# A two-direction state-space layer on Trainium2: whole-array decay tiles, B and C held once, more buffers, a smaller software DMA space

## The reference

```python
xn = _layernorm(x, axis=-1)
zxbcdt = xn @ in_proj_w.T           # z 2048, x 2048, B 64, C 64, dt 16 columns
def _branch(zxbcdt, conv_w, conv_b, dt_bias, A_log, D, norm_w):
    dt = softplus(zxbcdt[..., -NHEADS:] + dt_bias)
    A = -exp(A_log)
    xBC = silu(causal_conv(xBC, conv_w, conv_b))     # 4 taps over time
    # per head h of 16, head width 128, state width 64:
    #   h_t = h_{t-1} * exp(dt_t * A) + dt_t * x_t B_t ;  y_t = h_t C_t
    y = _ssd_scan(x, dt, A, Bm, Cm) + D * x
    yz = y * silu(z)
    return yz * rsqrt(mean(yz * yz) + EPS) * norm_w
y_fw = _branch(zxbcdt, ...)
y_bw = _branch(zxbcdt[:, ::-1, :], ...)              # the same, time reversed
s = (y_fw + y_bw[:, ::-1, :]) @ out_proj_w.T
g = silu(ffn(xn))     # ffn: 1024 x 1024 matmul, inputs and weights rounded to a 6-bit grid
x = x + s * g
```

## Time and profile before

| | us |
|---|---|
| median of 3 runs | 1595.62 |
| lowest and highest of them | 1593.83, 1722.22 |
| the profiled execution's own time | 1591.32 |
| its span on the slowest core (core 4) | 1589.8 |
| spans of the 8 cores | 1564.6 to 1589.8 |
| PE busy on that core | 1327.5 |
| DVE, ACT, POOL busy | 980.8, 831.1, 710.5 |

### The profile page before, as it was taken

One profiled execution on the slowest core, in us unless ns is written; L12 is line 12 of the kernel. 1 busy time (PEld: TensorE's weight loads), 2 busy tenths in 40 slices (PEclk: granted clock), 3 DMA queues, 4 the chain that ended last, 5 costly groups with the idle time before them and its releaser, 6 DMA issues.

```text
span 1589.8 us, 38392 instructions; the slowest of 8 cores (1564.6 to 1589.8 us)
## 1 busy us (share of the span) xinstructions
PE 1327.5 (84%) x13568; PEld 770.9 (48%) x13568; DVE 980.8 (62%) x1760; ACT 831.1 (52%) x1660; POOL 710.5 (45%) x950
## 2 busy tenths in 40 slices
PE   0677998977999899999896588898988889888995
PEld 0453665555655566656663343444444444444442
DVE  2615877665788876677745665654556655666652
ACT  0235665554656656665665654544445555555540
POOL 2422565543656545556432433453444444343442
PEclk9887998998999999999996699989999989998998
DMA  9793898989987877776688778998999888888862
GB/s 172 164 177 87 198 207 180 166 198 203 188 191 172 184 180 182 187 183 154 154 235 224 180 182 192 224 205 202 201 211 209 217 204 215 210 214 203 209 158 80
DMA packets 447284, 298.03 MB, mean 187 GB/s; under 512 B 321139, under 2 KB 395379, under 8 KB 445558
## 3 DMA queue, kind: packets, MB, share of 16 engines
q1 hardware_dynamic: 444502, 282.44, 75.4%
q0 software_dynamic: 2592, 13.14, 5.4%
HBM read 152.39 MB, written 84.94 MB: 149 GB/s over the span
## 4 chain that ended last, share of the span: by engine, by line
PE 51%; DMA 16%; ACT 10%; issue 9%; DVE 7%; SPq 5%; POOL 1%; DVEq 0%; ACTq 0%; POOLq 0%
PE ps L356 51%; SPq L383 5%; ACT L366 3%; DMA xtm<-cvx 3%; DMA g<-scr 3%; DMA ar<-yz 2%; DMA xt<-xn 2%; ACT e L366 2%; DMA u<-u 2%; DMA ar<-wz 2%; DVE yz L369 2%; DMA scr<-lts 1%; ACT sq L366 1%; DMA lts<-spl 1%; ACT cvx L366 1%
## 5 line engine op out<-in xcount | busy, mean ns | idle before, releaser
L356 PE MATMUL ps<-ar,xt 128*128 128x512 bf16 (+1 forms) x1792 | 379.9, 356 | 118.9 <-DMA xt<-xn 45.2
L356 PEld LDWEIGHTS ps<-ar,xt 128*128 128x128 bf16 x1792 | 148.8, 98 | 315.1 <-issue 172.2
L356 PE MATMUL ps<-xt,ar 128*128 128x256 bf16 x2304 | 277.9, 278 | 19.6 <-ACT stg L366 7.3
L366 ACT ACTIVATE cvx<-ps,cbt 128x256 bf16<-128x256 f32 x512 | 200.7, 474 | 175.5 <-PE ps L356 149.1
L356 PE MATMUL ps<-ar 128*128 128x512 bf16 x1024 | 259.5, 398 | 16.7 <-ACT e L366 12.7
L369 POOL TENSOR_TENSOR stmp<-st,dec 128x1024 f32<-128x1024 bf16 x64 | 132.7, 2074 | 292.0 <-DVE spl L380 120.6
L356 PEld LDWEIGHTS ps<-xt,ar 128*128 128x128 bf16 x2304 | 222.3, 100 | 63.8 <-issue 32.7
L369 DVE TENSOR_TENSOR yz<-ps,sz 128x1024 bf16<-128x1024 f32 x128 | 154.9, 1219 | 40.8 <-PE ps L356 40.5
L366 ACT ACTIVATE sq<-yz 128x1024 bf16<-128x1024 bf16 x128 | 134.9, 1054 | 78.0 <-DVE yz L369 34.8
L356 PE MATMUL ps<-stg,cd 64*64 64x256 bf16 x4096 | 157.8, 296 | 18.5 <-ACT cvx L366 6.6
L356 PEld LDWEIGHTS ps<-ar 128*128 128x128 bf16 x1024 | 95.1, 101 | 151.3 <-issue 59.6
(11 more groups left out here) (92 smaller groups left out, 1684.8 us busy)
## 6 DMA issues: line engine op xcount, KB each, us to landing
u<-u SPq DMA_DIRECT2D x54, 512.0 KB, 5.2
sp_x<-stg SPq DMA_DIRECT2D x64, 256.0 KB, 3.0
g<-scr SPq DMA_DIRECT2D x64, 256.0 KB, 5.3
sp_z<-sz SPq DMA_DIRECT2D x32, 512.0 KB, 4.3
sp_y<-yz SPq DMA_DIRECT2D x32, 512.0 KB, 5.0
sz<-sp_z SPq DMA_DIRECT2D x32, 512.0 KB, 4.5
ar<-sp_y SPq DMA_DIRECT2D x32, 512.0 KB, 4.6
stg<-sp_x SPq DMA_DIRECT2D x60, 259.0 KB, 4.6
```

The source lines that it names most:

```text
L356: return lambda e: e.matmul(out, lhsT, rhs, start=start, stop=stop)
L366: return lambda e: e.activation(out, in_, func, **kw)
```

## The change

1. **Decay tiles over the whole array.** `lts` now holds, per chunk and per half b of the moving tokens, a stationary tile of 128 columns (all 128 output tokens), and `rh` is one tile, not two. A call of `weights` still issues four matmuls, now of 128 stationary columns and 4 heads x 64 tokens = 256 moving columns. The mask is split: within a block of 64 by 64 tokens it stays in rows 64 to 127; the block that is masked altogether gets its -1e30 from two constant rows, 56 and 57. `spl` and the DMA transpose of it are half as wide; the transpose goes to a new tile `ltt`, from which a new DVE copy spreads 56 rows into `lts`. One DMA, not two, writes the rows of `rh`. `LTS.free` no longer waits for the store to `scr`.
2. **B and C once.** The projection gives 128 columns (B, C) in place of 256; the spilled array `sp_bc`, the tile `sbc`, the evacuation, the halo copies, the store and the load are half as large. The convolution's matmuls for them read the one copy, both column halves from the same rows.
3. **Buffers.** `E` 4 (was 3), `GC` 2 (was 1), `YB` 2 (was 1), `YT` 3 (was 2).
4. **Recording order in the second phase.** The load of `sp_y`, the add and the transpose of the sum are taken out of `b_scan` into `b_sum`, which is recorded after the output projection of the previous group.
5. **Software DMA space.** `dynamic_dma_scratch_size=8192` is passed when the program is built.

```diff
+        rh[d, 57 - d] = NEG
+        rh[d, 64:128] = np.tile(m[0:64, 0:64], (1, 2))[:, None, :]
+    c["c_rh"] = rh.reshape(2, 128, NH * 128)
+    lt = np.zeros((128, 2, 2, 128), dtype=BF)
+    lt[57, :, 0, 64:128] = 1.0
+    lt[56, :, 1, 0:64] = 1.0
+    for b in range(2):
+        lt[64:128, :, b, b * 64:(b + 1) * 64] = np.eye(64, dtype=BF)[:, None, :]
...
-    eb = [A(f"e{i}", [128, 1024], BF16) for i in range(3)]
-    gcb = [A("gc", [128, 1024], BF16)]
+    eb = [A(f"e{i}", [128, 1024], BF16) for i in range(4)]
+    gcb = [A(f"gc{i}", [128, 1024], BF16) for i in range(2)]
...
-        ti, lt, tfree = LTS.take()
-        t1 = dma("sp", f"lts{ti}", go(lt[:], sp[:].rearrange("p m f -> p (m f)").rearrange(
-            "p (m f) -> p m f", f=128), transpose=True), [parts, a5, tfree], 128, us=1.2,
+        ji, lj, jfree = LTT.take()
+        t1 = dma("sp", "ltt", go(lj[:], sp[:].rearrange("p c q f -> p (c q f)").rearrange(
+            "p (m f) -> p m f", f=128), transpose=True), [parts, a5, jfree], 64, us=1.2,
             rate=100.0)
...
+        ti, lt, tfree = LTS.take()
+        t3 = put("dve", cp(lt[0:56, :, :, :],
+                           lj[0:56, :, :].unsqueeze(2).broadcast_to([56, 2, 2, 128])), [t1, tfree],
+                 dve2(512))
+        LTT.give(ji, [t2, t3])
...
-        trh = [dma("sp", f"rh{hi}{a}", go(
-            rh[a][48:56, :], scr.rearrange("c (i h) t -> (c i) (h t)", i=4)),
-            [t2, hfree], 32, rate=20.0) for a in range(2)]
+        trh = dma("sp", "rh", go(
+            rh[48:56, :], scr.rearrange("c (i h) t -> (c i) (h t)", i=4)), [t2, hfree], 32,
+            rate=20.0)
...
-            for q in range(2):
-                o = hf * 1024 + q * 512
-                for a in range(2):
-                    steps.append(mm(sp[a * 64:(a + 1) * 64, q * 512:(q + 1) * 512],
-                                    dc["lt"][:, 2 * c, a * 64:(a + 1) * 64],
-                                    rh[a][:, o:o + 512], True, True))
+            sp3 = sp.rearrange("p (h t) -> p h t", h=8)
+            rh3 = rh[:].rearrange("p (h t) -> p h t", h=NH)
+            for b in range(2):
+                tb = slice(b * 64, (b + 1) * 64)
+                for q in range(2):
+                    o = hf * 8 + q * 4
+                    steps.append(mm(sp3[:, q * 4:(q + 1) * 4, tb], dc["lt"][:, c, b, :],
+                                    rh3[:, o:o + 4, tb], True, True))
...
+                            f, w = (r, i + j) if n == 4 else (j, 0)
                             steps.append(mm(banks[m * 64:(m + 1) * 64, at:at + G],
-                                            cd[r * 64:(r + 1) * 64, (t + i + j) * 4 + k, :],
-                                            src[r * 64:(r + 1) * 64, i + j, o:o + G],
+                                            cd[f * 64:(f + 1) * 64, (t + i + j) * 4 + k, :],
+                                            src[f * 64:(f + 1) * 64, w, o:o + G],
...
-        steps = []
-        for j in range(2):
-            for k in range(8):
-                steps.append(mm(pj[:, j * G:(j + 1) * G], wxb[8][:, k, j * 128:(j + 1) * 128],
-                                xt_[:, k, :], k == 0, k == 7))
-        p = put("pe", steps, [t_xt, k_wx[8], pfree], pe_us(16 * G))
+        steps = [mm(pj[:, 0:G], wxb[8][:, k, :], xt_[:, k, :], k == 0, k == 7) for k in range(8)]
+        p = put("pe", steps, [t_xt, k_wx[8], pfree], pe_us(8 * G))
...
-        "p (k t) -> p k t", k=16) for i in range(2)])
-    YB = Ring("yb", [ar[:, yb_o + i * 2048:yb_o + (i + 1) * 2048] for i in range(1)])
+        "p (k t) -> p k t", k=16) for i in range(2)]
+        + [ytb[:].rearrange("p (k t) -> p k t", k=16)])
+    YB = Ring("yb", [ar[:, yb_o:yb_o + 2048], ybb[:]])
...
+        return scans
+
+    def b_sum(g, scans):
+
+        for sc in scans:
             bi, yb, bfree = YB.take()
...
                 b_out(g - 1, old_scans[c], ffs[c], c)
+        b_sum(g, scans)
...
-    nc = bass.Bass("TRN2", target_bir_lowering=False)
+    nc = bass.Bass("TRN2", target_bir_lowering=False, dynamic_dma_scratch_size=8192)
```

82 lines of the change are left out of this document (41 added, 41 removed).

## The result

The changed kernel ran in 1589.36 us (median of 20 runs, 1570.03 to 1656.73), the kernel before beside it in 1596.98 us (20 runs). The ratio is 0.9933, 95% interval 0.9909 to 0.9957: 0.7% faster, which a threshold of 2% calls the same. Two later measurements gave 0.9902 (0.9866 to 0.9939) and 0.9939 (0.9904 to 0.9973). The forecast was 1558 us, 2.4% faster. Ratios and means leave out those executions, of either kernel, in which the cores of one die ran longer at a lower clock. The profiled execution is the luckiest of the twenty: 1570.03 us, span 1568.1. So its parts are compared with the earlier trace rows, but how much is gained is read from the many runs.

What follows compares the result with a forecast made beforehand. PE, busy 84% of the span, was taken as the bound. From 1591.3 us: 23 less for PE work, 18 less for buffers, 5 more for the copy gave 1555; half the 4.3 us median offset made 1558, range 1520 to 1592.

Steps and rivals of the forecast that it cites:

- The y buffer: Second phase: ending DVE's wait for `sp_y` cuts PE's four waits by a fifth, 12 us, plus 6 us of clock.
- PE work only: Rival: only removed PE work counts, since DVE's freed time was covered; 1573 to 1577 us, chance 0.26.
- `E` and `GC`: Scan buffers: only let PE interleave scan steps with other matmuls; no separate gain within 18 us for all buffers.
- B and C once: First-phase projection: eight matmuls fewer per group, 15.4 us of PE work; smaller evacuation and transfers costed at nothing.
- the 23: Both phases: PE work removed by decay tiles and single B and C that reaches the end, 23 us, between 15 and 29.
- Decay tiles: Decay matmuls, both phases: each of 128 sets of four 0.11 us shorter, 14 us of PE work.
- The busy time near 60 us: Sign in the profile: the row of 512 decay matmuls would show a busy time near 60 us.
- The copy's wait: New DVE copy: waits 20 to 40 us for the transpose, mainly before 400 us; copy and wait cost 5 us.
- The wider weight load: Rival: decay matmuls' 128-column weight loads take 224 ns and slow PE, 1610 us, chance 0.01.
- The software DMA space: POOL's weight loads at the start: the halved space costs 0, at most a few tens of us if too short.

Runs made afterwards that it cites:

- no_y: Changed kernel without the second y buffer, the third transposed y and the later sum; 0.9841 of the kernel before.
- y2_sum: Kernel before with only the second y buffer, the later sum and the smaller software DMA space; 1.0177 of the kernel before.
- bufs: Kernel before with only the extra exp, C times decay and y buffers, the later sum and the smaller software DMA space; 0.9953 of the kernel before.
- no_bufs: Changed kernel without the added buffers and the later sum, software DMA space as before; 0.9962 of the kernel before.
- e4gc2: Kernel before with a fourth exp buffer, a second C times decay buffer and the smaller software DMA space; 0.9981 of the kernel before.
- bc_once: Kernel before with only the single B and C, decay tiles and buffers as before; 0.9981 of the kernel before.
- no_bc: Changed kernel with B and C still made twice; 0.9973 of the kernel before.
- hold_before: Kernel before with the first z weight load held until the first group's second xd transpose has landed; 1.0049 of the kernel before.

## Why the prediction was wrong

The median fell by 7.6 us (18.1 and 7.8 in the two later measurements); the forecast of 1558 us lay 38 us under the median of 1595.6 shown before it. Its terms came to 36 us.

- **The y buffer (12 us and 6 of clock).** This step failed: that PE's four waits of the earlier trace rows shrink by a fifth once DVE no longer waits for `sp_y`. "DVE waits 68.6 us for `sp_y`" was true, the wait did go, and nothing was gained: PE's idle time from 900 to 1500 us grew from 81.1 to 91.5 us, `no_y` is as fast as the changed kernel or faster, and `y2_sum` is 17 us slower than before. The wait was one of several: behind it stood ACT's exponentials (59.9 us) and `g` (43.7), where the forecast had 20 to 30 us for `g`. The clock did rise, by more than was forecast (0.98), but `bufs` shows that little of this reaches the end. The rival "PE work only" said that DVE's freed time was covered and was closer, at 1573 to 1577.
- **`E` and `GC`.** The forecast gave them nothing of their own. They are what buffers give: `no_bufs` to `no_y` is 12.5 us by mean core (on two chips), and `e4gc2` alone 4.7; with one `GC` buffer the changed kernel, y part included, gains nothing. No wait of the earlier trace rows names that buffer.
- **B and C once (12 us of the 23).** The mechanism was right: 10.7 us less on the row (15.4 forecast), 0.82 us a group in `bc_once`. Its worth by mean core is 6 to 7 us beside the buffers and 0 to 20 elsewhere. What was not foreseen is that SP's transpose moves into the first z weight load, on some cores.
- **Decay tiles (11 us of the 23, 5 us back for the copy).** The size of the work was wrong: some 6 us by the steps (an estimate) and 4.2 by the row, in place of 14. The 0.11 us of the earlier trace rows came true, but only ahead of a whole-array matmul, which is what the earlier trace rows shows; the forecast took it for all 128 sets. Ahead of the 64-row convolution it is 0.02, and sets that stand two in a row were at 0.99 us for eight already. The busy time near 60 us that was to show it confused steps with durations. The net of 6 us lies by the 6 to 9 us measured in company, and that is luck: alone the same edit loses 10 us.
- **The copy's wait.** 18.7 us in total (forecast 20 to 40), 10.0 at most, 15.3 of it before 400 us; 13.7 us of work (11). Nearly as forecast. What it costs the end, 5 us in the sum, no run shows.
- **The wider weight load.** 100 ns a load, 48.5 us for 512, and no loss of PE time: that rival is out. By the Trainium skill (TensorE: Matmul & The Clock Gate, LDWEIGHTS) the load takes columns / 1.2 ns, 107 ns for 128 columns and 53 for 64. The trace's 100 ns is near the first, its 112 ns for 64 columns is twice the second; the measured durations decide.
- **The slowest core.** The forecast worked on one core's trace. By mean core the change gives 16 to 19 us; the slowest core lies 16 to 20 us above the mean in place of 12 to 14, which takes 3 to 6 us of it. Why it does is open: the stand at the start does not explain it, since `bc_once` has the stand on five cores and a distance of 12.5 us, `no_bc` and `hold_before` have none there and 19.3 and 18.7. The sum on the mean core was still 36 us: more than half of the miss would be there without the spread.
- **The software DMA space** was costed at nothing. POOL issued the eight `wx` loads in 4.35 us, without a stall; it was not tried alone, and in `bufs`, `y2_sum` and `e4gc2` it goes with the buffers.

## What to carry to other kernels

A long wait of an engine that is not the bottleneck is a sum over one releaser: before it is removed, look up what that instruction and the next ones wait for within the same microseconds, since the next wait takes its place. Try buffers one by one and in company: here the y part cost 17 us by itself, and beside it another buffer, which no wait named, decided whether anything was gained. Measure a step against every kind of neighbour that it will have. On several cores, read the first hundred microseconds on every core: an earlier start can move a queue's instruction into a long transfer on some cores only.

## What the runs showed of the hardware

**A tiny DVE instruction can take two microseconds beside POOL.** DVE's timeline of the changed kernel, core 3 (start us, us, what):

```profile
1174.48 0.17 DVE L391 CAST dec<-g 128x8 f32<-128x8 bf16 x1
1174.55 0.69 DVE L380 TENSOR_TENSOR gc<-g,cvb 128x1024 bf16<-128x1024 bf16 x1
1175.15 1.86 DVE L391 CAST dec<-g 128x8 f32<-128x8 bf16 x1
1176.93 2.46 DVE L384 TENSOR_SCALAR yz<-yz,rr 128x2048 bf16<-128x2048 bf16 x1
```

POOL's over the same microseconds:

```profile
1174.79 2.21 POOL L380 TENSOR_TENSOR stmp<-st,dec 128x1024 f32<-128x1024 bf16 x1 [2.98 <-DVE dec L391]
1176.95 1.89 POOL L380 TENSOR_TENSOR bw<-btm,w 128x1024 bf16<-128x1024 bf16 x1
```

The same cast takes 0.17 us and then 1.86: it ends at 1177.01, with POOL's first product (1177.00). The scaling begins then and ends at 1179.39, 0.5 us behind POOL's second product. The long casts came with the second `GC` buffer: all 64 casts together are busy 8.6 to 21.2 us in the seven kernels with one, the y part in or out, and 34.5 to 55.2 in the eleven with two; `gc1`, which takes only this buffer out of the changed kernel, has 21.2 in place of 55.0. With two, a product `gc` stands between the two casts of a group in DVE's order, while POOL's product, which waits for the first cast, starts; with one, the second cast follows the first at once. The Trainium skill (SBUF — State Buffer, SBUF: two separate sides) has VectorE and GpSimd take one shared port pair as an exclusive lock for a whole instruction. The two ends that coincide agree with it. No run here moved POOL's products alone, so the lock is a reading of the rows and not a test.

**A transpose that SP issues into a large load from POOL's queue can hold SP 10 to 27 us.** 20.82 us at 62.37 in the changed kernel, 1.48 us once the load was held; 25.77 us at 95.86 on a core of its third profile. In the 160 cores' traces of all twenty profiles 96 transposes took over 10 us, and each of them was issued 1.4 to 6.4 us behind a load from POOL's queue; with no such load issued in the 30 us before, none of 42,000 took more than 8.1 us, and half took under 1.3. When it strikes differs by core at the same program.
